# A cross-attention block on one core: three PSUM banks for the scores whose maximum is taken, one for the products with V

## What is computed

```python
# x: (8, 112, 256), context: (8, 375, 256), 16 heads of 16, all float32
Q = (x @ Wq.T + bq)        -> (8, 16, 112, 16)
K = (context @ Wk.T + bk)  -> (8, 16, 375, 16)
V = (context @ Wv.T + bv)  -> (8, 16, 375, 16)
attn = softmax(Q @ K^T / 4)                 # over the 375 keys
output = (attn @ V) @ W_o.T + b_o
y = layernorm(output + x) * gamma + beta    # eps 1e-5
```

## Time and profile before

| | us |
|---|---|
| median of 3 runs | 174.21 |
| lowest, highest | 173.33, 175.35 |
| the profiled execution, its own time | 175.05 |
| its span, first to last instruction | 173.2 |
| mean granted TensorE clock | 0.945 |

### The profile page before, as it was taken

One profiled execution on the slowest core, in us unless ns is written; L12 is line 12 of the kernel. 1 busy time (PEld: TensorE's weight loads), 2 busy tenths in 40 slices (PEclk: granted clock), 3 DMA queues, 4 the chain that ended last, 5 costly groups with the idle time before them and its releaser, 6 DMA issues.

```text
span 173.2 us, 3762 instructions
## 1 busy us (share of the span) xinstructions
PE 147.0 (85%) x1452; PEld 118.2 (68%) x1452; DVE 114.1 (66%) x254; ACT 80.4 (46%) x157; POOL 57.6 (33%) x65
## 2 busy tenths in 40 slices
PE   5959970987578999999999999999999899999830
PEld 4759850965276877988987888899776676566410
DVE  1465599479828786686878778787779869131242
ACT  3535740021013655654555474555656445766400
POOL 8961996006410088030224052113005005031141
PEclk9978997599969999999999999999999999999985
DMA  6967797000797918203700420071033000100000
GB/s 158 335 214 281 186 263 303 0 4 0 267 287 206 181 48 276 84 0 96 267 27 6 182 90 27 7 265 32 4 147 130 25 5 4 30 4 27 0 27 27
DMA packets 10817, 19.56 MB, mean 113 GB/s; under 512 B 1920, under 2 KB 6912, under 8 KB 10800
## 3 DMA queue, kind: packets, MB, share of 16 engines
q1 hardware_dynamic: 10208, 17.64, 31.3%
q0 software_dynamic: 592, 1.70, 4.1%
HBM read 6.30 MB, written 0.92 MB: 42 GB/s over the span
## 4 chain that ended last, share of the span: by engine, by line
PE 65%; DVE 21%; DMA 5%; issue 2%; POOL 2%; SPq 2%; ACT 2%; POOLq 0%; ACTq 0%; DVEq 0%
PE m_bank L676 19%; PE pv_bank L751 13%; PE mx_bank L719 12%; PE st_bank L737 12%; DVE mx L559 9%; PE m_bank L783 4%; DVE o_raw L608 3%; DMA x_raw<-xT 3%; PE m_bank L766 2%; DMA q_stack<-shift 2%; POOL xk L330 2%; DVE o_norm L586 1%; DVE xk L498 1%; DVE k_hl L527 1%; ACT xk L384 1%
## 5 line engine op out<-in xcount | busy, mean ns | idle before, releaser
L559 DVE TENSOR_REDUCE mx<-mx_bank 112x1 f32<-112x375 f32 x128 | 66.1, 541 | 24.4 <-PE mx_bank L719 23.8
L473 ACT ACTIVATE pw<-st_bank 125x448 f32<-125x448 f32 x96 | 52.2, 547 | 56.5 <-PE st_bank L737 56.4
L719 PE MATMUL mx_bank<-k_stack,q_stack 128*112 128x376 f32 x96 | 35.1, 387 | 10.6 <-DVE mx L559 10.1
L737 PE MATMUL st_bank<-q_stack,k_stack 128*125 128x224 f32 x144 | 30.8, 296 | 1.6 <-DMA q_stack<-shift 1.6
L719 PEld LDWEIGHTS mx_bank<-k_stack,q_stack 128*112 128x112 f32 x96 | 17.4, 186 | 17.1 <-DVE mx L559 16.6
L737 PEld LDWEIGHTS st_bank<-q_stack,k_stack 128*125 128x125 f32 x144 | 23.6, 188 | 6.2 <-issue 4.5
L751 PE MATMUL pv_bank<-pw,v_sb 125*17 125x112 f32 x768 | 27.5, 262 | 0.0
L676 PE MATMUL m_bank<-w_hl,c_hl 128*125 128x256 f32 x144 | 21.9, 294 | 0.3 <-DVE k_hl L527 0.3
L676 PEld LDWEIGHTS m_bank<-w_hl,c_hl 128*125 128x125 f32 x144 | 20.6, 199 | 0.9 <-DVE k_hl L527 0.6
L676 PE MATMUL m_bank<-c_hl,w_hl 128*128 128x376 f32 x96 | 20.8, 359 | 0.2 <-DVE c_hl L509 0.2
L353 POOL TENSOR_SCALAR var_eps<-mv 112x1 f32<-112x1 f32 x8 | 1.8, 224 | 56.5 <-DVE mv L599 56.5
(11 more groups left out here) (67 smaller groups left out, 154.8 us busy)
## 6 DMA issues: line engine op xcount, KB each, us to landing
k_stack<-k_hl SPq DMA_DIRECT2D x18, 376.0 KB, 3.6
c_raw<-ctxT SPq DMA_DIRECT2D x8, 375.0 KB, 4.0
xk<-k_hl SPq DMA_DIRECT2D x6, 376.0 KB, 3.0
q_stack<-q_hl SPq DMA_DIRECT2D x6, 224.0 KB, 9.7
q_stack<-q_hl SPq DMA_DIRECT2D x6, 168.0 KB, 3.3
x_raw<-xT SPq DMA_DIRECT2D x2, 448.0 KB, 5.6
xb<-x_nat POOLq DMA_DIRECT2D x1, 896.0 KB, 13.9
out<-yo SPq DMA_DIRECT2D x8, 112.0 KB, 1.9
```

Source lines behind the costliest of these rows:

```text
L473: nc.scalar.activation(p_tile[0:KC, n % PR, :, :], st_bank[n % 2][0:KC, 0:4 * Q].rearrange("p (j q) -> p j q", j=4), ACT.Exp, scale=float( ...
L559: nc.vector.tensor_reduce(mx[b % 2][:, h % 2, h // 2:h // 2 + 1], mx_bank[n % 2][0:Q, 0:KV], axis=AX_X, op=ALU.max).then_inc(max_read, 1)
L719: nc.tensor.matmul(mx_bank[n % 2][0:Q, 0:KVP], q_stack[k][:, side, h // 2, b - Q_STACKS[k][0], :], k_stack[b % 3][:, h // 2, :], start=Tru ...
L737: last = nc.tensor.matmul(st_bank[n % 2][0:KC, k * 2 * Q:(k + 1) * 2 * Q], k_stack[i % 3][:, 2 * g + k, c * KC:(c + 1) * KC], q_stack[qk][ ...
```

## The change

The scores for the maximum get three banks in place of two, so that a head waits for the reduction of the head three before it. The products with V get one bank in place of two, so that group 0 of each batch from 1 on waits for the copy of the batch just before it; one memset of a bank goes.

```diff
+MR = 3
...
-        mx_bank = [bank(f"mx_bank{i}") for i in range(2)]
-        pv_bank = [bank(f"pv_bank{i}") for i in range(2)]
+        mx_bank = [bank(f"mx_bank{i}") for i in range(MR)]
+        pv_bank = bank("pv_bank")
...
-                nc.scalar.copy(o_raw[b % 2][:, :], pv_bank[b % 2][:, 0:NG * Q]).then_inc(o_raw_ready, 1)
+                nc.scalar.copy(o_raw[b % 2][:, :], pv_bank[:, 0:NG * Q]).then_inc(o_raw_ready, 1)
...
-            for i in range(2):
-                nc.vector.memset(pv_bank[i][:, :], 0.0).then_inc(pv_clear, 1)
+            nc.vector.memset(pv_bank[:, :], 0.0).then_inc(pv_clear, 1)
...
-                nc.vector.tensor_reduce(mx[b % 2][:, h % 2, h // 2:h // 2 + 1], mx_bank[n % 2][0:Q, 0:KV],
+                nc.vector.tensor_reduce(mx[b % 2][:, h % 2, h // 2:h // 2 + 1], mx_bank[n % MR][0:Q, 0:KV],
...
-                if n >= 2:
-                    pe.wait_ge(max_read, n - 1)
+                if n >= MR:
+                    pe.wait_ge(max_read, n - MR + 1)
...
-                nc.tensor.matmul(mx_bank[n % 2][0:Q, 0:KVP],
+                nc.tensor.matmul(mx_bank[n % MR][0:Q, 0:KVP],
...
-                    if b >= 2:
-                        pe.wait_ge(o_raw_ready, b - 1)
+                    if b >= 1:
+                        pe.wait_ge(o_raw_ready, b)
...
-                        last = nc.tensor.matmul(pv_bank[b % 2][32 * j:32 * j + VW, g * Q:(g + 1) * Q],
+                        last = nc.tensor.matmul(pv_bank[32 * j:32 * j + VW, g * Q:(g + 1) * Q],
...
-            pe.wait_ge(pv_clear, 2)
+            pe.wait_ge(pv_clear, 1)
```

## The result

The changed kernel takes 169.17 us (median of 4 runs, 168.6 to 169.77); the kernel before took 174.78 beside it. The ratio is 0.9706, 95% interval 0.9619 to 0.9794: 3% faster. The forecast was 168.4, 5.8 us less than before; the profiled execution lost 5.45 us of its own time (175.05 to 169.60) and 5.4 of its span (173.2 to 167.8).

A forecast was written before the change was run, and what follows sets the result against it. PE was taken as the bound almost everywhere in the loop, short of buffers rather than speed. Gains of 8.0 us less 2.2 lost gave 5.8 net: 169.25 us profiled, 168.4 us median, range 165.8 to 172.0.

The forecast's parts named there:

- Before the loop: Start up to the shift DMA: V and heads wait less, last Q projection 2.1 us earlier; bounds 0.8 and 2.7.
- Batch 0: Crowded DVE, three heads a unit: fewer weight-load waits, 1.2 us gained, bounds 0.4 and 1.8; unit 7's 0.5 counted separately.
- My 0.5 us of loss for V at the low clock: Before the loop: one more V projection falls before the clock rises, 0.5 us taken off the gain.
- Unit 0 of batch 1 and units 7 of batches 1 to 4: PE's stand of 0.5 us at each goes; with batch 0's unit 7, six stands, 3.0 us gained.
- Unit 9: PE's five stands of 0.2 to 0.3 us counted at nothing, since V then waits for DVE's copy of the transposed maximum.
- Batches 5 and 6: No projections, DVE the nearer bound: 1.4 us gained, bounds 0.3 and 2.3, and one more stand of 0.3 in batch 6.
- the stands: Unit 2 of batches 6 and 7: PE's products with V wait for ACT's copy, 2.2 us lost, bounds 1.6 and 2.6.
- rival (c): Slower: the clock falls behind the two new stands in batches 6 and 7, 1.4 us more each; 176.0 us, chance 0.06.
- (a): Across the kernel, DVE takes the freed time: only 2.3 us net gain, 171.9 us, chance 0.18.
- (b): The clock stays at 2.4 GHz around 48 to 52 us, 1.4 us won, plus 0.5 of units 9; 166.5 us, chance 0.16.

The follow-up runs named there:

- e2: Changed kernel with the third bank used only before the loop, two-bank waits from head 22 on; median 175.69 us against 175.28 for the kernel before.
- e5: Changed kernel with two-bank waits for heads 0 to 21 and three banks only in the loop; ratio 0.9794 to the kernel before.
- e6: Changed kernel with its bank for the products with V cleared twice; ratio 0.9623 to the kernel before.
- e3: Changed kernel with ACT's copy of the V bank ahead of unit 2's exponential in batches 6 and 7; ratio 0.9583 to the kernel before.
- e4: Changed kernel with V's last chunk in unit 10 in place of 9; ratio 0.9741 to the kernel before.
- e1: Kernel before with one bank for the products with V, scores for the maximum still in two; ratio 1.0198 to the kernel before.
- e8: e3 with DVE's copy of the shift (transposed maximum) ahead of unit 8's first reduction; ratio 0.945 to the kernel before.
- e10: Changed kernel with two filler matmuls ahead of PE's wait for ACT's copy in batch 7; ratio 0.9677 to the kernel before.
- e11: Changed kernel once more, without filler, beside e10; ratio 0.9753 to the kernel before.
- e9: e8 with DVE's copy of the V bias moved behind the reduction of head 9; ratio 0.921 to the kernel before.

## Why the prediction was right

**Before the loop: 2.1 us forecast, 1.9 to 3.2 measured.** What released V, how the memset, the K DMAs and the shift DMA moved, and that the removed memset is worth nothing all stand as forecast; e2, e5 and e6 part them. V's first projection started 6.93 us behind POOL's memset and 8.37 before: 1.44 us, where 1.4 was forecast. The size of the whole hangs on the clock. With the clock low for 6.8 us around this stretch, as before, e3 and e4 took 24.37 and 24.25 us from memset to batch 0, 1.9 and 2.0 less than 26.24, and 2.4 to 2.5 less than e1 and e5, which have the start of before and took 26.77 and 26.78. With 3.4 us of it, in the changed kernel, e2, e6, e8, e10 and e11, it is 2.9 to 3.2, above my upper bound of 2.7. V now runs in the gap in which PE stood idle, and in most of these executions the clock rose 3.4 us sooner; whether the earlier work brings that about or the moment of the execution was not parted. My 0.5 us of loss for V at the low clock was right in the first case and a gain missed in the second.

**Batch 0: 1.2 + 0.5 forecast, 1.9 measured** in the one pair of profiles. Here too the clock counts: it is low around the wait for the shift DMA, in some executions for 3.4 us and in others for 6.8. Like with like, batch 0 took 17.37 us before and 15.47 to 15.57 in the changed kernel, e6, e10 and e11 (3.4 us), and 17.62 and 17.60 in e1 and e2 against 16.23, 16.26 and 16.00 in e3, e4 and e5 (6.8 us): 1.3 to 1.9 us.

**Unit 0 of batch 1 and units 7 of batches 1 to 4: 2.5 forecast, 2.55 measured. Unit 9: nothing forecast, nothing gained.** The last is the step I am surest of now: e8 shows that 0.3 us a batch was to be had there, by moving what stands behind the wait, and e4 that moving the wrong side of it makes it worse.

**Batches 5 and 6: 1.4 and 0.3 forecast.** Batch 5 gained 1.46, and 1.1 us of waits remain there, four of them:

```profile
PEld mx_bank L719 <- DVE mx L559: 1.1, 4, 0.4
```

Batch 6 with the stands came out at +1.96, where 2.2 - 0.3 = 1.9 was forecast, and e1 has the stands alone at 2.26.

**The clock behind the stand: the term that was missing.** I priced the stands at 2.2 us, let the clock fall there in rival (c) only, and argued against it by the length of the stands. In the seven profiles of kernels with the full stand in batch 7 (the changed one, e1, e2, e4, e5, e6, e11) it fell behind it in six, 1.4 to 2.1 us behind its end: 1.4 us lost in five, 4.9 in e1. In the three with a stand of 0.4 us (e3, e8, e9) and in e10, where filler stands in it, it didn't fall there. Between e10 and e11 only the filler differs, so it points to the idle array, as far as one profile a side goes; that e2 had the stand and kept its clock shows that the stand alone doesn't settle it. The start of the kernel tells the same: in eleven of the twelve profiles PE stands 3.7 to 5.4 us before the loop, and the clock falls within this stand or at most 0.6 us behind its end; e9, which has no such stand, is at 2.4 GHz from 15.7 to 39.6 us. The Trainium skill, "TensorE: Matmul & The Clock Gate", tells in its section "A second HAM failure mode: psum-queue depth-cycling" of a kernel whose clock swung with short idle times between groups of matmuls. The many waits of the ring did not (1.00 in the earlier trace rows); the one stand of 1.15 us in batch 7 mostly did.

**The total, and what of it was luck.** Counted from POOL's memset to PE's last matmul the profile gained 5.77 us where 5.8 was forecast. That it agrees so well is luck: 1.4 us were lost behind the stand of batch 7, 1.1 more than forecast were won before the loop, where the clock has a part too; batch 0 gave 0.2 more and the other stages come within 0.1 of their forecasts together. The forecast for the profiled execution was 169.25 us and 169.60 came, since the memset itself began 0.4 us later. The other 0.4 of the 0.8 us between 168.4 and 169.17 is the step from profile to median, for which I took 0.84 us from the runs of before; here it was 0.43.

**The rivals.** (a), DVE takes the freed time, fell: half the units 7 would have been 0.25 us a batch, and it was 0.5. It was true of one place, unit 9. (b) didn't come true in its place: from 45 to 52 us the mean granted clock was 0.76 in the changed kernel and 0.76 before. What the clock gave came earlier, from 28 to 35 us, 0.76 in place of 0.52. (c) had the mechanism right in one of its two places and the sum wrong, since the gains were 9 us and not 3.

## What to carry to other kernels

Price a ring of buffers at each place from start to start of the matmuls, not by the idle time in brackets, and look one instruction behind each wait that goes: the next wait is often there already, and moving the work of the releasing engine (e8) pays where moving the waiting work (e4) doesn't. When a second buffer is given up, its price is set where the order of the work is tightest, here two handovers of seven, and an instruction that waits in front of the copy (the exponential) can double it; putting the copy first took back 1.5 us, and in none of the three profiles with it did the clock fall right behind the stand. A wait for one engine may be a third engine's doing: DVE's 5 us were POOL's memset.

## What the runs showed of the hardware

- DVE's copy of a float32 column in SBUF beside a POOL memset: the two took 5.20 us before, 5.44 and 4.62 with more and less of the memset ahead of them, each time until the memset's end or 0.1 us behind it, and 0.34 us in e9 with the memset over. Low parts and reductions, whose main input is PSUM, were not held: in e9 a low part took its 0.61 us in the middle of the memset. The Trainium skill, "SBUF — State Buffer", says in its section "Who interferes with whom" that VectorE and GpSimd take turns on a shared pair of ports, which one instruction holds to its end, and that copies are among the operations that can want it; the three traces with the copy held, and e9 with it out of the way, agree.
- The clock fell from 2.4 to 1.2 GHz a little after PE had stood for 1.15 us in batch 7, and not after stands of 0.42 us there, nor after the one of 0.98 us in batch 6, nor in e2. It also fell within, or at most 0.6 us behind, the stand of 3.7 to 5.4 us before the loop, in all eleven profiles that have one. How long it stayed low behind the stand of batch 7 differed from execution to execution, 3.4 us in five and 10.2 in one; so the price of such a stand is no one number, and I had none in my sum.
